# Moving a head's pair products from the start of the next step into the tail of its own step, in a kernel with a gated delta rule, a sparse graph mix and a mixture of experts

## The chip, the cores and the metric

The kernel runs on one core of a Trainium2 chip. The core has five engines that run their own instruction streams and meet only at semaphores: TensorE (PE: matmuls and transposes, PEld is its weight load), VectorE (DVE), ScalarE (ACT), GpSimd (POOL) and SyncE (SP), which here issues the DMAs. The metric is the time of one execution on the device in microseconds; the median of several runs counts.

## What is computed

x is (4, 256, 256). One decoder layer in three parts, each added to x after a layer norm:

```python
# 1: gated delta rule, 8 heads of 128, two Householder steps (j) per token
q, k, v = causal_conv_silu(x @ Wq), causal_conv_silu(x @ Wk), causal_conv_silu(x @ Wv)
q = l2norm(q) / sqrt(128); k = l2norm(k); beta = 2 * sigmoid(x @ Wb)
g = -exp(A_log) * softplus(x @ Wa + dt_bias)
for t in range(256):
    state = state * exp(g[t])
    for j in range(2):
        u = (v[t, j] - k[t, j] @ state) * beta[t, j]
        state = state + outer(k[t, j], u)
    o[t] = q[t] @ state
x = x + (rmsnorm(o) * norm_w * silu(x @ Wg)) @ Wo
# 2: top-k masked sigmoid of a similarity of ctx_512 (4, 256, 64), k = 76 of 256, symmetrised, mixed with norm(x)
# 3: feed forward: base expert plus the top 2 of 8 experts, hidden 704
```

## The kernel before, in words

The whole layer is float32 and runs in one program: `attention` (parts 1 and 2, about the first 630 us) and `feed_forward` (the rest). The diff touches `attention` alone.

**Chunks.** Time is cut into 4 chunks of 64 steps, that is 128 Householder rows; 4 sequences times 4 chunks make 16 tiles (BC) for each head. Inside a tile the recurrence is solved with the inverse of a 128x128 triangular matrix. Its strictly triangular part is `aT` (products of keys, times decays and beta, the array `dx`); its inverse is `TT`. The four 32x32 diagonal blocks of all 16 tiles are sent through device memory (`gather`: eight DMAs aT to a_blocks, then two a_blocks to `blk`), so that GpSimd can invert the 64 blocks side by side in 31 rounds of two instructions (`invert`, lines 1370 and 1373), and come back with `scatter` (inv to inverses, inverses to TT). TensorE then joins the blocks in five levels, each for two halves of the tiles (`p32`, `t32`, `x32`, `p64`, `t64`), and ScalarE copies each level out of PSUM.

**Steps.** The eight heads go through a software pipeline with four stages. In step s stage A works on head s (projections, convolution, norms, decays), B on head s-1 (inverse, transposes), C on head s-2 (the scan over four chunks) and E on head s-3 (output projection). There are 11 steps, 0 to 10. Each step has 12 slots and a place behind them, LAST; before the change it also had a place ahead of them, FIRST. A table, `FILL`, says which items of A, B and E stand in which place. The order in the code is the order on each engine; nothing reorders it.

**Items and banks.** An item is a group of matmuls into one of three PSUM banks (`bankB`) in rotation, so an item waits until the one three places before it in the table has been copied out (`bank_free`). `pair` n (8 of them for a head) makes the key and query products of two tiles; VectorE turns each into `aT` (line 1121) and `mq` (the masked query products, line 1126), 0.4 and 0.3 us. `dx`, `ex` are decays and `out` is the output projection, whose result VectorE adds to `acc` (line 1214) times `factor`, the inverse root mean square of the head's output. `factor` is made in three places: TensorE's `out_sums` (line 725) at the start of the step, VectorE's `out_rms` (lines 1204, 1206), GpSimd's `out_rms` (line 1300), and the first `out` item of the step waits for it.

**Slots.** Slot i has projection i (line 582, slots 0 to 9) on TensorE, convolution i-1 (line 1055, three instructions, slots 1 to 10) on VectorE, and one third of a scan chunk: products with the state S (line 683, slots 3, 6, 9), with TT (697, slots 1, 4, 7, 10), with the query and the state update (711 to 716, slots 2, 5, 8, 11). VectorE makes R (1154), U (1162, also printed R) and S (1169, 1171) between them. The selection of the top 76 of each row (`topk`, lines 1070 and 1072, 20 calls for a tile of rows) fills VectorE's holes in steps 2 to 8: calls 0 to 7 in slot 0, calls 8 to 19 in slot 11. `turn_blocks` (line 1144, X1 from TT) is in slot 9 and waits for the DMAs of `scatter`; `p32` in slot 10 needs X1. At the end of a step ScalarE squares the output (`out_square`, line 889) and VectorE gates it (`out_gate`, line 1197).

On GpSimd the step is: clear TT, reset `inv` (`unit`), copy the head's conv weights and make `gm` (`start`), `out_rms`, `invert`, and then, for the head in A, `dm`, beta into `dx`, `kn`, `sh` and `qE`.

Of the kernel before, what the change touches and what calls it, by code (L numbers as in the profile page):

```python
# [98 lines left out]
def four(kind):  # L99
# [62 lines left out]
def attention(nc, ctx, t, dram):  # L162
# [45 lines left out]
    mq = [sb(f"mq{i}", [P, BATCH, CH, STEPS]) for i in range(2)]  # L208
    gate = [sb(f"gate{i}", [P, T]) for i in range(2)]
# [46 lines left out]
    m8 = sb("m8", [P, 8])  # L256
    thr = t["thr"]
# [128 lines left out]
    def sync_program(sp):  # L386
# [34 lines left out]
        def tiles_out():  # L421
# [112 lines left out]
    def tensor_program(pe):  # L534
# [80 lines left out]
        def item(kind, n, X):  # L615
# [12 lines left out]
            if kind in ("pair", "vtok", "kend"):  # L628
# [1389 lines left out]
```

## Time and profile before

| | |
|---|---|
| time, median of 3 runs | 946.38 us (941.20, 946.38, 946.81) |
| the profiled execution, its time | 940.37 us |
| its span, first to last instruction | 938.3 us |
| PE busy | 835.7 us (89%) |
| DVE, ACT, POOL busy | 530.1, 390.9, 347.5 us |
| mean granted TensorE clock | 0.939 |
| share of PE in the chain that ended last | 72% |

The span is some 2 us shorter than the time of that execution. The granted clock of TensorE is a share of 2.4 GHz; 0.50 is the lower level, 1.2 GHz. Busy time of a group counts each instruction once; the idle time in brackets at a row is the time in which that engine had nothing running just before the row, with the work that ended it.

### The profile page before, as it was taken

What the parts mean: (1) busy time and instruction counts of PE and PEld (TensorE: products, weight loads), DVE (VectorE), ACT (ScalarE), POOL (GpSimd) and SP (SyncE); (2) the same over time, 40 slices, a digit from 0 to 9 for tenths busy, and PEclk for the clock granted to TensorE, in tenths of its full rate; (3) what the DMA queues carried; (4) which work ended last, traced back from release to release, by engine and by line L of the source; (5) the groups of instructions that cost most, each with busy time, mean ns of one, the idle gap of its engine ahead of it and who ended that gap; (6) DMA issues with size and microseconds to landing.
All of it is one profiled execution on the core that took longest, in us unless ns stands there. A gap on an engine that the chain in (4) does not pass through costs nothing.

```text
span 938.3 us, 16243 instructions
## 1 busy us (share of the span) xinstructions
PE 835.7 (89%) x5560; PEld 580.5 (62%) x5561; DVE 530.1 (56%) x1285; ACT 390.9 (42%) x839; POOL 347.5 (37%) x654
## 2 busy tenths in 40 slices
PE   3969999989999999899899876874999999999992
PEld 2343566756766756767667765663667667666761
DVE  4564757878878868878778755465511111111113
ACT  3536756545654554655555323202222222222220
POOL 0157368457456565563683580003330000000015
PEclk9788999999999999999999886897999999999997
DMA  7302230130031031021201301009563100110104
GB/s 204 78 12 56 69 85 1 24 80 12 13 80 23 7 74 22 14 68 24 51 1 24 83 9 29 1 1 384 215 228 129 34 28 28 34 34 22 34 25 127
DMA packets 102593, 57.88 MB, mean 62 GB/s; under 512 B 64192, under 2 KB 98048, under 8 KB 102528
## 3 DMA queue, kind: packets, MB, share of 16 engines
q1 hardware_dynamic: 99488, 51.62, 20.0%
q0 software_dynamic: 1536, 4.20, 1.4%
q10 hardware_dynamic: 1504, 1.20, 0.4%
q8 instruction: 39, 0.64, 0.3%
q14 instruction: 26, 0.21, 0.1%
HBM read 42.45 MB, written 14.55 MB: 61 GB/s over the span
## 4 chain that ended last, share of the span: by engine, by line
PE 72%; DVE 10%; ACT 5%; POOL 4%; issue 4%; DMA 3%; SPq 1%; ACTq 0%; POOLq 0%; DVEq 0%
PE bank L1599 16%; PE bank L582 11%; PE bank L1644 9%; PE bank L712 3%; PE bank L590 3%; PE bank L637 3%; DVE y L1055 3%; PE bank L746 2%; PE bank L716 2%; PE bank L711 2%; PE bank L697 2%; PE bank L1631 2%; PE bank L596 2%; PE bank L671 2%; PE bank L683 2%
## 5 line engine op out<-in xcount | busy, mean ns | idle before, releaser
L1055 DVE SCALAR_TENSOR_TENSOR y<-bank,cwh,y 128x510 f32<-128x510 f32 (+2 forms) x240 | 177.5, 743 | 82.5 <-ACT y L833 78.8
L582 PE MATMUL bank<-xnT,wbuf 128*128 128x512 f32 x320 | 164.8, 641 | 5.5 <-DVE y L1055 5.0
L1599 PE MATMUL bank<-f_wgu,f_xgT 128*128 x368 | 118.8, 466 | 0.0
L1858 DVE TENSOR_TENSOR f_act<-f_sg,bank 128x352 f32<-128x352 f32 x62 | 32.2, 521 | 139.8 <-PE bank L1599 135.1
L1370 POOL TENSOR_TENSOR term<-inv,blk 128x126 f32<-128x126 f32 (+22 forms) x248 | 87.4, 352 | 63.3 <-DMA blk<-a_blocks 44.5
L1933 POOL DMA_INDIRECT f_back<-slots_y,f_slot x16 | 15.4, 960 | 228.8 <-DMA slots_y<-f_yb 222.2
L582 PEld LDWEIGHTS bank<-xnT,wbuf 128*128 128x128 f32 x320 | 56.8, 197 | 67.4 <-issue 53.8
L1373 POOL TENSOR_TENSOR inv<-inv,term 128x126 f32<-128x126 f32 (+22 forms) x248 | 91.2, 368 | 19.4
L1706 ACT ACTIVATE f_sg<-bank 128x352 f32<-128x352 f32 x62 | 28.6, 463 | 158.7 <-PE bank L1599 158.7
L1644 PE MATMUL bank<-f_wdn,f_actT 128*128 (+1 forms) x372 | 91.5, 387 | 0.8 <-ACT f_actT L1719 0.8
L1599 PEld LDWEIGHTS bank<-f_wgu,f_xgT 128*128 128x128 f32 x368 | 66.2, 190 | 36.8 <-issue 7.6
L833 ACT ACTIVATE y<-bank,cwh 128x512 f32<-128x512 f32 x80 | 54.9, 686 | 75.1 <-PE bank L582 73.4
L1644 PEld LDWEIGHTS bank<-f_wdn,f_actT 128*128 128x128 f32 x372 | 67.9, 189 | 24.1 <-issue 11.3
L1315 POOL TENSOR_TENSOR dx<-dx,minus_beta 128x1024 f32<-128x1024 f32 x8 | 15.2, 1902 | 115.6 <-DVE beta_n L1105 115.6
L637 PE MATMUL bank<-kq 128*128 128x192 f32 x256 | 47.3, 342 | 8.5 <-DVE mq L1126 8.5
L712 PE MATMUL bank<-mq,R 128*128 128x64 f32 x256 | 48.2, 288 | 3.1 <-DVE R L1162 3.1
L637 PEld LDWEIGHTS bank<-kq 128*128 128x128 f32 x256 | 43.2, 197 | 11.1 <-DVE mq L1126 10.2
L932 ACT ACTIVATE vtok<-bank,kn 128x128 f32<-128x128 f32 x128 | 36.4, 369 | 32.3 <-PE bank L642 32.3
L1300 POOL TENSOR_TENSOR factor<-factor,masks 128x8 f32<-128x8 f32 x8 | 13.3, 1662 | 85.7 <-DVE factor L1206 85.7
L1599 PE MATMUL bank<-f_wgu,f_x2T 128*128 128x352 f32 x128 | 44.4, 494 | 0.4 <-DVE f_act L1858 0.4
L712 PEld LDWEIGHTS bank<-mq,R 128*128 128x128 f32 x256 | 40.1, 205 | 6.6 <-DVE R L1162 3.7
L596 PE MATMUL bank<-gm,masks 64*128 64x512 f32 x64 | 30.2, 747 | 12.7 <-ACT dx L872 7.2
(204 smaller groups left out, 1501.4 us busy)
## 6 DMA issues: line engine op xcount, KB each, us to landing
f_wgu<-in_exp_gu SPq DMA_DIRECT2D x8, 1408.0 KB, 8.7
f_wdn<-in_exp_dn SPq DMA_DIRECT2D x8, 640.0 KB, 9.3
blk<-a_blocks SPq DMA_DIRECT2D x16, 256.0 KB, 3.9
slots_x<-oT SPq DMA_DIRECT2D x24, 128.0 KB, 1.9
f_xg<-slots_x SPq DMA_DIRECT2D x24, 128.0 KB, 2.0
slots_y<-f_yb SPq DMA_DIRECT2D x23, 128.0 KB, 1.7
a_blocks<-aT SPq DMA_DIRECT2D x64, 32.0 KB, 1.6
inverses<-inv SPq DMA_DIRECT2D x16, 128.0 KB, 3.0
```

The lines of the kernel that those rows point to most:

```text
L582: last = mm(bankA[p % 2][:, :], wbuf[A.par][:, kt, wblk, :], xnT[:, kt, (p % 2) * 512:(p % 2 + 1) * 512], start=kt == 0, stop=kt == 1)
L596: return mm(bank[:, :], mask("rest" if kind == "dx" else "ones", i * STEPS, STEPS), gm[half_, :, :].rearrange("p n t -> p (n t)"), start=T ...
L637: last = mm(bank[:, c * (MU + STEPS):(c + 1) * (MU + STEPS)], kraw[:, 2 * n + c, :], kq[:, 2 * n + c, :], start=True, stop=True)
L712: last = mm(out, U[:, b, :], mq[par][:, b, c, :], start=c == 0, stop=True)
L833: a(y[p % 2][:, :, :].rearrange("p b t -> p (b t)"), bankA[p % 2][:, :], ACT.Copy, scale=cwh[A.par][:, cb, 3:4]).then_inc(evac_done, 1)
L932: last = a(vtok[B.par][:, b, c, :], bank[:, c * P:(c + 1) * P], ACT.Copy, scale=kn[:, b * CH + c:b * CH + c + 1])
L1055: v.scalar_tensor_tensor(out=y[p % 2][:, :, k:], in0=src[:, :, 0:SEQ - k], scalar=cwh[A.par][:, cb, 3 - k:4 - k], in1=y[p % 2][:, :, k:], ...
L1370: g.tensor_tensor(step_term, inv[:, 0:r, j:j + 1].to_broadcast([P, r, k]), blk[:, j:j + 1, j + 1:].to_broadcast([P, r, k]), ALU.mult).then ...
L1373: g.tensor_tensor(inv[:, 0:r, j + 1:], inv[:, 0:r, j + 1:], step_term, ALU.add).then_inc(inv_done if j == NB - 2 else inv_step, 1)
L1599: last = mm(gu[c][:, 0:FFH], xt[:, k, :], wgu[:, e, k, at:at + FFH], start=k == 0, stop=k == 1)
L1644: last = mm(dn[par][:, 0:HID], aT[0:rows, par, k, :], wdn[0:rows, e, k, :], start=k == 0, stop=k == FT - 1)
L1858: v.tensor_tensor(av[:, par, half * FFH:(half + 1) * FFH], sg[:, half, :], gu[2 * half + 1][:, 0:FFH], ALU.mult).then_inc(f_act, 1)
```

## The change

The pair products of a head no longer open the next step. They stand in the head's own step: pairs 0 and 1 in slot 10, 2 and 3 in slot 11, and 4 to 7 in LAST, between the level products of the head ahead. `aT` has two buffers, since the level products of one head and the pair products of the next are now interleaved. The masked decays, which had the array `dm`, are written straight into one of three rotating `mq` buffers and multiplied in place. `gather` stands at the end of a head's own step. The decays' second half `ex` moves to slot 1; the squares and norms move earlier, and VectorE's norm sum and beta from slot 10 to slot 8. `turn_blocks` moves from slot 9 to slot 7, the levels up to `x32` 0 one place ahead. The selection makes 14 calls in slot 0 and the last 6 after LAST. On GpSimd `start`, `unit` and `clear` of the next inverse stand in the step before, and `out_rms` stands inside `invert`, ahead of round 12 (`RMS_AT`). Step 0 and step 8 have entries of their own.

```diff
-FIRST, LAST = "first", "last"
-FILL = {FIRST: {"B": [("pair", n) for n in range(BC // 2)]},
-        0: {"A": [("dx", 0), ("dx", 1), ("ex", 0), ("ex", 1)]},
-        1: {"E": [("out", 0)], "B": [("vtok", 0)]},
+LAST = "last"
+FILL = {0: {"A": [("dx", 0), ("dx", 1)]},
+        1: {"A": [("ex", 0), ("ex", 1)], "E": [("out", 0)], "B": [("vtok", 0)]},
...
-        8: {"B": [("kend", 1)]},
-        9: {"B": [("gate", 0)]},
-        10: {"B": [("p32", 0), ("p32", 1)], "E": [("out", 3)]},
-        11: {"B": [("t32", 0), ("t32", 1), ("kend", 2)]},
-        LAST: {"B": [("x32", 0), ("x32", 1), ("gate", 1), ("p64", 0), ("p64", 1), ("t64", 0), ("t64", 1)]}}
+        8: {"B": [("kend", 1), ("gate", 0)]},
+        9: {"B": [("p32", 0), ("p32", 1), ("kend", 2)]},
+        10: {"B": [("t32", 0), ("t32", 1)], "A": [("pair", 0), ("pair", 1)]},
+        11: {"B": [("x32", 0)], "A": [("pair", 2), ("pair", 3)], "E": [("out", 3)]},
+        LAST: [("B", [("x32", 1)]), ("A", [("pair", 4), ("pair", 5)]), ("B", [("p64", 0), ("p64", 1), ("gate", 1)]),
+               ("A", [("pair", 6), ("pair", 7)]), ("B", [("t64", 0), ("t64", 1)])]}
+
+STEP_0 = {0: {}, 1: {}, 3: {"A": [("dx", 0), ("dx", 1), ("ex", 0), ("ex", 1)]}}
...
+RMS_AT = 12
+TOP_FIRST = 14
...
         def step(A, B, C, E):
-            if B:
-                gather(B)
...
+            if A:
+                gather(A)
...
-                if A and 6 <= slot < 10:
-                    norm(A, slot - 6)
+                if A and slot in (5, 7):
+                    norm(A, slot - 5)
+                    norm(A, slot - 4)
...
-                if A and 5 <= slot <= 10:
-                    square(A, slot - 5)
+                if A and slot in (4, 6, 8):
+                    square(A, slot - 4)
+                    square(A, slot - 3)
...
-                    topk(tiles[0], 0, 8)
+                    topk(tiles[0], 0, TOP_FIRST)
...
-                if B and slot == 9:
+                if B and slot == (7 if A else 10):
                     turn_blocks(B)
-                if A and slot == 10:
+                if A and slot == 8:
                     norm_sum(A, 0)
                     fold_beta(A)
...
             fill(LAST)
+            if A and tiles:
+                topk(tiles[0], TOP_FIRST, 2 * ROUNDS)
...
             for j in range(NB - 1):
+                if j == RMS_AT and E:
+                    out_rms(E)
...
             if B:
-                clear(B)
-                unit(B)
-            if A:
-                start(A)
-            if E:
+                invert(B, E)
+            elif E:
                 out_rms(E)
-            if B:
-                invert(B)
             if A:
...
                 decays(A)
+                if A.h + 1 < HEADS:
+                    start(Head(A.h + 1, (A.h + 1) % 2, (A.h + 1) // 2))
+                if A.h:
+                    unit(A)
                 fold_beta(A)
                 norm(A)
                 scalars(A)
                 q_decay(A)
+                clear(A)
```

TensorE at the boundary of two steps, before. L669 is `x32`, L590 the gate, L671 `p64`, L673 `t64`, L637 the pairs, L725 `out_sums`, L596 the decays, L582 projection 0:

```order
L669 MATMUL bank<-masks,TT 64x64 x16
L590 MATMUL bank<-xnT,wg 128x512 x2
L671 MATMUL bank<-XP,aT 64x64 x16
L673 MATMUL bank<-TT,XP 64x64 x16
L637 MATMUL bank<-kq 128x192 x16
L725 MATMUL bank<-osq,masks 32x256 x4
L596 MATMUL bank<-gm,masks 128x512 x4
L582 MATMUL bank<-xnT,wbuf 128x512 x2
```

The same place after. L693 is `x32`, L652 the pairs, L770 `out`, L626 the norms, L695 `p64`, L605 the gate, L697 `t64`, L749 `out_sums`, L611 the decays:

```order
L693 MATMUL bank<-masks,TT 64x64 x8
L652 MATMUL bank<-kq 128x192 x4
L770 MATMUL bank<-wo,og 128x256 x2
L626 MATMUL bank<-osq,masks 32x128 x8
L693 MATMUL bank<-masks,TT 64x64 x8
L652 MATMUL bank<-kq 128x192 x4
L695 MATMUL bank<-XP,aT 64x64 x16
L605 MATMUL bank<-xnT,wg 128x512 x2
L652 MATMUL bank<-kq 128x192 x4
L697 MATMUL bank<-TT,XP 64x64 x16
L749 MATMUL bank<-osq,masks 32x256 x4
L611 MATMUL bank<-gm,masks 128x512 x2
```

The 16 pair matmuls that stood between `t64` and `out_sums` are in groups of four ahead of `t64`, so `out_sums` now follows `t64` directly.

GpSimd at the start of a step with all four stages, before. L1300 is `out_rms`, L1370 and L1373 are the rounds of `invert`:

```order
L1347 MEMSET TT 128x16x32
L1354 MEMSET inv 128x512
L1358 AFFINE_SELECT inv<-inv 64x512 x2
L1281 COPY cwh<-cw 128x20
L1287 TENSOR_TENSOR gm<-g_sb,masks 128x512
L1300 TENSOR_TENSOR factor<-factor,masks 128x8
L1370 TENSOR_TENSOR term<-inv,blk 128x31
L1373 TENSOR_TENSOR inv<-inv,term 128x31
```

After. L1322 is `out_rms`, L1395 and L1398 the rounds:

```order
L1398 TENSOR_TENSOR inv<-inv,term 128x6x21
L1395 TENSOR_TENSOR term<-inv,blk 128x120
L1398 TENSOR_TENSOR inv<-inv,term 128x6x20
L1322 TENSOR_TENSOR factor<-factor,masks 128x8
L1395 TENSOR_TENSOR term<-inv,blk 128x133
L1398 TENSOR_TENSOR inv<-inv,term 128x7x19
```

`out_rms` has moved behind twelve of the 31 rounds, so it also stands behind their wait for `blk`.

VectorE between slots 7 and 9, before. L1144 is `turn_blocks`, L1171 makes S, L1154 R, L1055 are convolutions, L1214 the addition of `out`:

```order
L1171 SCALAR_TENSOR_TENSOR S<-S,sh,bank 128x128 x4
L1055 SCALAR_TENSOR_TENSOR y<-bank,cwh,y 128x2x254
L1055 SCALAR_TENSOR_TENSOR y<-bank,cwh,y 128x2x253
L1132 TENSOR_TENSOR kend<-bank,sh 128x4x128
L1055 SCALAR_TENSOR_TENSOR y<-bank,cwh,y 128x2x255
L1154 SCALAR_TENSOR_TENSOR R<-bank,sh,vtok 128x128 x4
L1055 SCALAR_TENSOR_TENSOR y<-bank,cwh,y 128x2x254
L1055 SCALAR_TENSOR_TENSOR y<-bank,cwh,y 128x2x253
L1144 STREAM_TRANSPOSE X<-TT 32x512 x2
```

After. L1167 is `turn_blocks`, L1194 makes S, L1079 are convolutions, L1237 the addition of `out`, L1107 opens the norm sum:

```order
L1237 SCALAR_TENSOR_TENSOR acc<-bank,factor,acc 128x256 x2
L1167 STREAM_TRANSPOSE X<-TT 32x512 x2
L1079 SCALAR_TENSOR_TENSOR y<-bank,cwh,y 128x2x255
L1194 SCALAR_TENSOR_TENSOR S<-S,sh,bank 128x128 x4
L1079 SCALAR_TENSOR_TENSOR y<-bank,cwh,y 128x2x254
L1079 SCALAR_TENSOR_TENSOR y<-bank,cwh,y 128x2x253
L1155 TENSOR_TENSOR kend<-bank,sh 128x4x128
L1107 STREAM_TRANSPOSE turned<-bank 128x512
```

`turn_blocks` now stands ahead of convolution 7 and of the third update of S.

## Rows read from the trace of the kernel before

**Rows 1.** The page: its first line, its part 1 and the clock of its part 2.

```profile
span 938.3 us, 16243 instructions
...
PE 835.7 (89%) x5560; PEld 580.5 (62%) x5561; DVE 530.1 (56%) x1285; ACT 390.9 (42%) x839; POOL 347.5 (37%) x654
...
PEclk9788999999999999999999886897999999999997
```

**Rows 2.** Windows (length, busy us of PE, PEld, DVE, ACT, POOL, clock, DMA): steps 4, 5, 8.

```profile
258.20:323.90 65.70, 62.78 (x533) 44.42 (x533) 54.58 (x127) 37.50 (x74) 38.42 (x77) 1.00 0.18 37
323.90:391.20 67.30, 64.41 (x533) 44.91 (x533) 54.50 (x127) 37.42 (x74) 38.43 (x76) 0.97 0.17 37
524.40:598.00 73.60, 54.16 (x436) 45.35 (x437) 38.98 (x118) 21.44 (x43) 23.95 (x64) 0.74 0.16 38
```

**Rows 3.** Timeline of PE, step 5 (start, length, what).

```profile
320.31 2.22 PE L637 MATMUL bank<-kq 128*128 128x192 f32 x12
323.86 3.52 PE L637 MATMUL bank<-kq 128*128 128x192 f32 x20 [1.33 <-DVE mq L1126]
...
330.97 1.12 PE L596 MATMUL bank<-gm,masks 64*128 64x512 f32 x2 [1.11 <-ACT dx L872]
...
343.39 1.05 PE L683 MATMUL bank<-S,kT 128*128 128x128 f32 x8
...
368.75 1.05 PE L683 MATMUL bank<-S,kT 128*128 128x128 f32 x8
...
385.67 2.04 PE L673 MATMUL bank<-TT,XP 64*64 64x64 f32 x32
```

**Rows 4.** Timeline of DVE, step 5.

```profile
327.41 0.42 DVE L1121 TENSOR_TENSOR aT<-bank,dx 128x256 f32<-128x256 f32 x1
...
328.58 0.42 DVE L1070 MAX8 m<-simw 128x8 f32<-128x256 f32 x1
...
336.37 0.75 DVE L1055 SCALAR_TENSOR_TENSOR y<-bank,cwh,y 128x510 f32<-128x510 f32 x1 [3.89 <-ACT y L833]
...
339.06 0.87 DVE L1214 SCALAR_TENSOR_TENSOR acc<-bank,factor,acc 128x256 f32<-128x256 f32 x2
...
341.43 0.88 DVE L1169 COPY S<-bank 128x128 f32<-128x128 f32 x4 [0.32 <-PE bank L716]
...
372.80 1.43 DVE L1144 STREAM_TRANSPOSE X<-TT 32x512 f32<-32x512 f32 x2
...
389.32 1.28 DVE L1197 SCALAR_TENSOR_TENSOR og<-oT,normw,gate 128x1024 f32<-128x1024 f32 x1 [0.82 <-ACT osq L889]
```

**Rows 5.** Timeline of POOL, step 5.

```profile
328.74 1.64 POOL L1300 TENSOR_TENSOR factor<-factor,masks 128x8 f32<-128x8 f32 x1 [3.63 <-DVE factor L1206]
336.64 0.24 POOL L1370 TENSOR_TENSOR term<-inv,blk 128x31 f32<-128x31 f32 x1 [6.26 <-DMA blk<-a_blocks]
...
346.67 0.42 POOL L1370 TENSOR_TENSOR term<-inv,blk 128x133 f32<-128x133 f32 x1
...
363.52 0.23 POOL L1373 TENSOR_TENSOR inv<-inv,term 128x16 f32<-128x16 f32 x1
```

**Rows 6.** The chain that ended last, step 2 (start, length, what).

```profile
164.88 4.28 DMA inverses<-inv
...
172.96 0.70 DVE X L1144
```

**Rows 7.** Timeline of PE, steps 8 and 9.

```profile
533.71 1.97 PE L712 MATMUL bank<-mq,R 128*128 128x64 f32 x8 [2.79 <-DVE R L1162]
...
575.43 1.92 PE L663 MATMUL bank<-X,aT 32*32 32x32 f32 x64 [7.20 <-DVE X L1144]
...
596.90 0.64 PE L725 MATMUL bank<-osq,masks 128*32 128x256 f32 x8 [1.63 <-ACT osq L889]
```

**Rows 8.** Window of step 8, columns as in rows 2.

```profile
538.00:540.00 2.00, 1.88 (x9) 1.54 (x8) 0.41 (x3) 1.14 (x4) 1.61 (x6) 0.50 0.93 314
```

**Rows 9.** Timeline of PE, step 1.

```profile
71.08 3.75 PE L596 MATMUL bank<-gm,masks 64*128 64x512 f32 x6 [5.10 <-POOL gm L1287]
```

More of the change, by code:

```diff
@@ L130, in items_at @@
     if step == 0:
-        table = FILL[0] if place == FIRST_DECAYS else {} if place == 0 else table
-    return table.items()
+        table = STEP_0.get(place, table)
+    if step == HEADS:
+        table = STEP_8.get(place, table)
+    return table.items() if isinstance(table, dict) else table
 def tiles_of(step):
@@ L256, in attention @@
     m8 = sb("m8", [P, 8])
+    aT1 = sb("aT1", [P, BATCH, CH, MU])
+    aT = [aT0, aT1]
     thr = t["thr"]
@@ L644, in item, with level_ready @@
                 return
+            level_ready(kind, n, h)
+            for k in range(BC // 2):
+                last = level(kind, n, X, k, bank)
+            last.then_inc(b_mm, 1)
+        def level_ready(kind, n, h):
             if kind == "p32":
@@ L674, in item, with level @@
-            last.then_inc(b_mm, 1)
+        def level(kind, n, X, k, bank):
+            par, m = X.par, n * (BC // 2) + k
+            a_m, t_m = aT[par][:, m // CH, m % CH, :], TT[par][:, m // CH, m % CH, :]
+            cols = slice(k * STEPS, (k + 1) * STEPS)
+            if kind == "p32":
+                for g in range(2):
+                    src, out = slice(2 * g * NB, (2 * g + 1) * NB), slice((2 * g + 1) * NB, (2 * g + 2) * NB)
+                    last = mm(bank[out, k * NB:(k + 1) * NB], a_m[src, out], X1[src, m, :], start=True, stop=True)
+            elif kind == "t32":
+                for g in range(2):
+                    src, out = slice((2 * g + 1) * NB, (2 * g + 2) * NB), slice(2 * g * NB, (2 * g + 1) * NB)
+                    last = mm(bank[out, k * NB:(k + 1) * NB], P32[src, m, :], t_m[src, src], start=True, stop=True)
+            elif kind == "x32":
+                last = nc.tensor.transpose(bank[0:64, cols], t_m[0:64, 0:64], ident[0:64, 0:64])
+            elif kind == "p64":
+                last = mm(bank[64:128, cols], a_m[0:64, 64:128], XP[0:64, m, :], start=True, stop=True)
+            else:
+                last = mm(bank[0:64, cols], XP[64:128, m, :], t_m[64:128, 64:128], start=True, stop=True)
+            return last
@@ L711, in scan @@
                         mm(out, S[:, b, :], qE[par][:, b, c, :], start=True, stop=False)
-                    last = mm(out, U[:, b, :], mq[par][:, b, c, :], start=c == 0, stop=True)
+                    last = mm(out, U[:, b, :], mq[h % 3][:, b, c, :], start=c == 0, stop=True)
                 last.then_inc(o_mm, 1)
@@ L756, in fill @@
                             item(kind, n, stages[stage])
-            fill(FIRST)
             if E:
@@ L1282, in start @@
                           cw[:, :, :, :].rearrange("p h a k -> p h (a k)")[:, h, :]).then_inc(cwh_done, 1)
-            if some(4 * h):
+            if h:
                 item_done(pool, "ex", h - 1, 1)
```

66 lines of the change are left out of this document (26 added, 40 removed).

## The prediction

> **What bounds the kernel now.** I read the page first, for which engine is near its limit [rows 1]: PE is busy 89% of the span and DVE only 56%. Then the windows by step, for where PE is not busy [rows 2]: the steps with all stages last 65.7 and 67.3 us in turn, mean 66.5, with PE busy for 62.8 and 64.4, so there are some 2.9 us to be had in each of them. Step 8, which has no projections, is another matter: 73.6 us, of which PE is busy 54 at a mean clock of 0.74. Last the timelines, to see who waits at the boundary of two steps. The gaps of PE there are 1.33 us, where a pair product waits for its bank, and 1.11 us, where a decay does [rows 3]. So the middle of the kernel is bound by TensorE with 96% filled, and a reordering can gain little there and lose much. The feed forward part is not touched.
>
> Below, S is the moment at which PE ends the last `t64` of a step: 387.71 (385.67 + 2.04), and 320.3 one step earlier, where the pairs begin [rows 3].
>
> **The pairs move ahead of S: nothing at first.** Their work is the same, 2.22 + 3.52 = 5.7 us [rows 3], and the two steps' starts shift by it. Between level products their banks have time to be read, so the wait of 1.33 us should go. What is late next is `out_sums`: it follows `t64` directly now, and needs ScalarE's square of the output, which ScalarE does only after the copy of the last `t64`. In step 9, the one step of before with no pairs in front, PE waited 1.63 us for just that [rows 7]. DVE's gate waits for the same square, and starts at 389.32, that is S + 1.6 [rows 4]. So 1.6 us comes for 1.33 us that goes. The 1.11 us of the decays should go too, because a projection now stands between `dx` and `ex`.
>
> **The inverse starts too late for its new place.** The inverse's round trip begins with the last `aT`. In step 5 that ends at 327.83 (327.41 + 0.42) [rows 4], and the first round starts at 336.64 [rows 5]: 8.8 us for `gather` and `blk`. The last pairs stand just ahead of `t64` (2.0 us) in the new order and their copy takes 0.4, so the last `aT` ends at about S - 1.6, and the first round starts at S + 7.2. Round 12 (133 wide) is 346.67 - 336.64 = 10.0 us further on [rows 5]. There GpSimd now makes `factor`, 1.64 us [rows 5]: it is ready at S + 18.9. Before, it was made ahead of the inverse, in time that GpSimd spent waiting for `blk` anyway (idle 6.26 us before the first round [rows 5]), at 330.4.
>
> When does VectorE want it? Gate from S + 1.6 to S + 2.8 (the 1.28 us row), 0.6 us for `out_rms`, then 14 calls of the selection in place of 8. Eight calls ran from 328.58 to 332.48 (336.37 less the idle time of 3.89) [rows 4], 0.49 us each, so 14 take 6.9 us and end at S + 10.3. One convolution, U and two convolutions lie between that and the addition of `out` 0: 339.06 - 336.37 = 2.7 us [rows 4], S + 13.0. Two costs follow. U comes to PE at S + 11.7; with two projections and the items of slot 1 done PE is there some 2 us earlier (estimate), a wait that the next one swallows. And DVE stops dead at the addition from S + 13.0 to S + 18.9, with convolution 1 and S queued behind it. Addition 0.8, convolution 0.7, S 0.9: S is ready at S + 21.3, and the third slot's product (line 683) can start. All of the earlier work of PE is long done by then.
>
> From that product to the end of `t64` PE ran without holes in step 5: 387.71 - 343.39 = 44.3 us, and the 5.7 us of pairs are added to it: the next S is 21.3 + 44.3 + 5.7 = 71.3 us after this one, against 66.5: **+4.8 us a step** if the clock stays up.
>
> **The clock.** After a wait of 2.79 us in step 8 PE ran at 0.50 of its clock [rows 7, 8]: eight product rows took 1.97 us, and the lower level, 1.2 GHz, was still on at 540. That is 6.3 us at half rate with 3.1 us lost; with what lies behind 540 I take 3.4. In the steps of now, the two small gaps cost 1.7 us every second step (clock 0.97 against 1.00 [rows 2]). The new waits, 1.6, 2 and up to 5 us, come within 21 us in each step. Some of the slow stretch falls into time in which PE waits anyway, so I take half of 3.4: 73.0 us a step, **+6.5**. The Trainium skill, page "TensorE: Matmul & The Clock Gate", section "What's actually happening", says that the throttled state is the default and that only activity releases it. By that rule PE would come out of every one of these waits at the low level, and the whole 3.4 us would be lost in each step: 74.7. No run of before shows such a wait inside a full step.
>
> Steps 3 to 7 have both a head in A and one in E: 5 x 6.5 = **+32**.
>
> **The way back.** From the last `aT` to X1 before: 8.8, then the rounds until 363.75, 27.1 us, then the DMAs, 172.96 - 164.88 = 8.1 and an issue of 0.6 [rows 5, 6]: 44 to 45 us. Slot 9 was reached at 372.80, 45.0 after 327.83 [rows 4], so this was just hidden. Now `turn_blocks` stands two slots earlier; VectorE reaches it about S + 42 in a held step and TT lands at S + 43.5 to 45 with the 1.6 us of `factor` added. That wait is small and mostly covered, because X1 is not used before slot 9, which PE reaches at 21.3 + (368.75 - 343.39) + 1.9 for the gate moved ahead of it = S + 48.6 [rows 3].
>
> **Step 2** has no head in E and so no hold, and there the round trip itself sets the length: X1 comes at 44 after the last `aT`, S 3.1 us later, then 387.71 - 368.75 = 19.0 from slot 9's product, less 1.9 for the gate, plus 5.7 for pairs, less 1.5 from S back to the last `aT`: 44 + 24.4 = 68.5, against the mean of 66.5, and 1.7 for low clock after the wait at `turn_blocks`: **+4**.
>
> **Steps 0 and 1.** `gm` is ready a step ahead: the wait of 5.10 us for it [rows 9] goes, and head 0's pairs can be done some 2 us sooner. But step 1 is bound by the round trip of head 0, and X1 in slot 7 holds convolutions 7 to 9 and the pairs behind it, where before only one convolution came after it: **+1**, bounds -5 and +3.
>
> **Step 8.** `factor` holds S in the same way. Before, S was made from about 537.5 (533.71 + 1.97, and as much again for the state update), 9.6 after the end of the pairs at 527.9 (524.4 + 3.5) [rows 2, 3, 7]; now from S + 19.7, +10. Only 6 instead of 12 calls of the selection stand on the way to slot 9, -2.9, and `turn_blocks` has U ahead of it, +0.7: **+8**, bounds +2 (no hold) and +10. The 7.20 us wait for X1 [rows 7] stays, since the selection and not the inverse ends last before it.
>
> Selection calls after LAST (2.9 us) fit between the last pair and the gate's wait. The array `mq` in three buffers, `aT` in two and the earlier squares and norms cost nothing: the same instructions, ahead of a user that comes later.
>
> **Sum**: 1 + 4 + 32 + 8 = +45 us on the profiled execution's 940.4: 985. The median of the three runs is 946.4, 6 above it, so I add 1: **986 us**. A change within 1% could not be told from none here.
>
> **Rivals.**
> 1. The hold is as forecast and each wait costs the full slow stretch (the skill's rule, as a mechanism of this kernel: PE resumes at 0.50 as in rows 8): 5 x 8.2 + 1 + 5 + 10 = +57, 997. For it: both long waits of step 8 went that way. Against: part of it falls into waits.
> 2. `factor` does not hold (if `blk` lands early, or the addition comes late). Then the round trip with `turn_blocks` in slot 7 sets the step: 44 + 1.7 + 24.4 = 70.1, 5 x 3.6 = 18, plus 5 and 3: 967.
> 3. Faster. The two gaps of PE go, its clock stays at 1.00, step 1 loses its 5.10 us, and step 8 has its inverse early: 7 x 1.3 + 6 x 0.85 + 6 + 8 = -28, 912. It decides at one point: `blk` has to be there by S - 1 and not S + 7.2, so that `factor` is ready when VectorE comes to it. For it: DVE and POOL have 40% and more to spare on average. Against: the last pairs are issued 2 us before S, and 8.8 us of DMA follow in every step of before.
> 4. Gains of steps 0, 1 and 8 and smaller holds cancel: within 1%.
>
> **How the numbers follow.** Forecast 0.45 (975 to 996), rival 1 0.20 (to 1003), rival 2 0.15 (958 to 974), rival 4 0.07, rival 3 0.10, worse than 1003 0.03. The range 958 to 1003 leaves out 0.20. Faster 0.10, same 0.07, slower 0.83.
>
> **What would show it.** Right: DVE's longest waits in steps 3 to 7 are at the addition of `out` 0 (line 1237) for GpSimd's `factor`, some 5 to 6 us each; PE waits 4 to 5 us at line 707 in slot 3 for S, and 1.6 us at line 749 for ScalarE; step length 71 to 75 us; low clock after slot 3. Wrong: `factor` ready before S + 13, a step below 67 us, or a first round earlier than 8 us after the last `aT`. The forecast fails most easily if VectorE's 14 calls or PE's path are already later than the hold, which would make the hold free.

## The result, and the profile after

The changed kernel takes 977.59 us (median of 4 runs, 973.46 to 981.35), the kernel before 945.95 in the same comparison. The ratio is 1.034, 95% interval 1.029 to 1.039: slower, by 31.6 us. The forecast was 986 with 958 to 1003.

The page of after, its first line, part 1 and clock, against [rows 1]:

```profile
span 976.3 us, 16235 instructions
...
PE 838.5 (86%) x5560; PEld 587.1 (60%) x5561; DVE 521.5 (53%) x1285; ACT 389.3 (40%) x839; POOL 341.6 (35%) x654
...
PEclk9999598998998998989989969797899999999997
```

The span is 38.0 us longer and PE is busy for only 2.8 us more, so the loss is in the main waiting. (The profiled execution of before was one of its faster ones, 940.4 us against a median of 946, which is why 38.0 is more than the 31.6 of the medians.) `t64` now ends a step, so S itself is the border. Windows of after, steps 3, 5 and 8 and two short stretches of step 5, columns as in [rows 2]:

```profile
203.28:274.52 71.24, 65.39 (x532) 46.42 (x532) 53.31 (x126) 37.30 (x73) 37.38 (x76) 0.93 0.17 34
346.05:418.35 72.30, 65.02 (x532) 46.40 (x532) 53.41 (x126) 37.43 (x73) 37.41 (x76) 0.93 0.17 34
561.33:631.30 69.97, 46.95 (x404) 39.78 (x404) 35.93 (x108) 23.28 (x46) 23.86 (x63) 0.76 0.16 38
367.64:370.64 3.00, 3.00 (x13) 3.00 (x14) 2.88 (x7) 0.03 (x1) 2.60 (x6) 0.50 0.00 0
370.64:373.64 3.00, 3.00 (x11) 1.51 (x11) 1.64 (x3) 2.21 (x6) 2.53 (x7) 0.77 0.00 0
```

The mean of steps 3 to 7 is (561.33 - 203.28) / 5 = 71.6 us. Before, from one end of `t64` to the next, it was 66.8. Three timelines of step 5 of after, with S = 346.05, answer to [rows 3, 4, 5]. PE:

```profile
343.97 2.08 PE L697 MATMUL bank<-TT,XP 64*64 64x64 f32 x32
347.67 0.71 PE L749 MATMUL bank<-osq,masks 128*32 128x256 f32 x8 [1.63 <-ACT osq L913]
...
357.89 1.00 PE L736 MATMUL bank<-mq,R 128*128 128x64 f32 x8
...
367.64 2.08 PE L707 MATMUL bank<-S,kT 128*128 128x128 f32 x8 [5.65 <-DVE S L1192]
```

DVE:

```profile
344.08 0.42 DVE L1145 TENSOR_TENSOR aT<-bank,dx 128x256 f32<-128x256 f32 x1
...
357.43 1.52 DVE L1079 SCALAR_TENSOR_TENSOR y<-bank,cwh,y 128x508 f32<-128x508 f32 x2
365.27 0.88 DVE L1237 SCALAR_TENSOR_TENSOR acc<-bank,factor,acc 128x256 f32<-128x256 f32 x2 [6.31 <-POOL factor L1322]
366.06 0.74 DVE L1079 SCALAR_TENSOR_TENSOR y<-bank,cwh,y 128x510 f32<-128x510 f32 x1
366.72 0.87 DVE L1192 COPY S<-bank 128x128 f32<-128x128 f32 x4
```

POOL:

```profile
353.61 0.24 POOL L1395 TENSOR_TENSOR term<-inv,blk 128x31 f32<-128x31 f32 x1 [17.21 <-DMA blk<-a_blocks]
...
363.12 0.44 POOL L1398 TENSOR_TENSOR inv<-inv,term 128x120 f32<-128x120 f32 x1
363.52 1.65 POOL L1322 TENSOR_TENSOR factor<-factor,masks 128x8 f32<-128x8 f32 x1
```

Read backwards, the three are one chain. PE stands for 5.65 us at the product of slot 3 until VectorE has made S. VectorE has stood for 6.31 at the addition of `out` 0, two instructions ahead of S, until GpSimd has `factor`. GpSimd made `factor` directly behind round 11 (no idle time in front of it), and its first round had waited for `blk`, whose data left with the last `aT` at 344.50. When PE resumes, eight products take 2.08 us at clock 0.50, where they took 1.05 in [rows 3]. The list of waits of after (total us, times, longest) says how often; the 6.6 us at line 736 are in step 2:

```profile
POOL term L1395 <- DMA blk<-a_blocks: 119.2, 8, 17.2
DVE acc L1237 <- POOL factor L1322: 36.2, 8, 7.1
PE bank L707 <- DVE S L1192: 27.7, 7, 5.7
PE bank L736 <- DVE R L1185: 11.5, 3, 6.6
```

**Where the 38.0 us lie.** Before, a step's own work began when the pairs were done. These two rows of PE before, and 527.96 for step 8 (524.44 + 3.52), give the starts; 595.28 ends step 8:

```profile
123.40 5.47 PE L637 MATMUL bank<-kq 128*128 128x192 f32 x32
...
190.87 3.52 PE L637 MATMUL bank<-kq 128*128 128x192 f32 x20 [1.79 <-DVE mq L1126]
...
593.23 2.05 PE L673 MATMUL bank<-TT,XP 64*64 64x64 f32 x32
```

| stretch | before | after | more | forecast |
|---|---|---|---|---|
| up to the end of step 1 | 128.87 | 134.85 | +6.0 | +1 |
| step 2 | 65.5 | 68.4 | +2.9 | +4 |
| steps 3 to 7 | 333.6 | 358.05 | +24.5 | +32 |
| step 8 | 67.3 | 70.0 | +2.7 | +8 |
| steps 9, 10 and feed forward | 343.0 | 345.0 | +2.0 | 0 |

Each column is one execution, and two rows of it scatter from one execution to the next. The last row, from the last `t64` to the end, is 343.0 to 343.2 in e1, e2, e3 and e9 and 347.8 and 348.7 in e8 and e12 (the runs below), all of which have the same instructions there as after; so its +2.0 need not be the change's. The first row has up to 3.5 us of such scatter (see steps 0 and 1 below).

### The profile page after: what moved, and what is told of

It reads as the page before. It is cut to its first block, busy times and chain, and to the rows that moved or that the text cites. A ratio compares the mean times of both kernels' runs of the same rounds, so it can differ in the third digit from the quotient of the medians.

```text
span 976.3 us, 16235 instructions
## 1 busy us (share of the span) xinstructions
PE 838.5 (86%) x5560; PEld 587.1 (60%) x5561; DVE 521.5 (53%) x1285; ACT 389.3 (40%) x839; POOL 341.6 (35%) x654
## 3 DMA queue, kind: packets, MB, share of 16 engines
q1 hardware_dynamic: 99488, 51.62, 19.4%
## 4 chain that ended last, share of the span: by engine, by line
PE 64%; DVE 8%; POOL 7%; DMA 5%; issue 3%; SPq 1%; ACT 1%; DVEq 0%; ACTq 0%
PE bank L1626 15%; PE bank L1671 8%; PE bank L597 8%; PE bank L652 4%; PE bank L707 3%; POOL inv L1398 3%; PE bank L605 3%; DMA blk<-a_blocks 3%; POOL term L1395 3%; PE bank L736 2%; PE bank L735 2%; PE bank L721 2%; PE bank L770 2%; PE bank L1658 2%; PE bank L740 2%
## 5 line engine op out<-in xcount | busy, mean ns | idle before, releaser
L1079 DVE SCALAR_TENSOR_TENSOR y<-bank,cwh,y 128x510 f32<-128x510 f32 (+2 forms) x240 | 177.6, 743 | 41.4 <-ACT y L857 37.4
L1395 POOL TENSOR_TENSOR term<-inv,blk 128x126 f32<-128x126 f32 (+22 forms) x248 | 87.4, 352 | 137.5 <-DMA blk<-a_blocks 119.2
L597 PEld LDWEIGHTS bank<-xnT,wbuf 128*128 128x128 f32 x320 | 61.2, 208 | 71.5 <-issue 58.1
L1398 POOL TENSOR_TENSOR inv<-inv,term 128x126 f32<-128x126 f32 (+22 forms) x248 | 91.1, 367 | 19.4
L1733 ACT ACTIVATE f_sg<-bank 128x352 f32<-128x352 f32 x62 | 28.6, 463 | 161.1 <-PE bank L1626 161.1
L707 PE MATMUL bank<-S,kT 128*128 128x128 f32 x192 | 32.6, 322 | 31.2 <-DVE S L1192 27.7
L707 PEld LDWEIGHTS bank<-S,kT 128*128 128x128 f32 x192 | 28.7, 225 | 41.5 <-DVE S L1192 32.4
L652 PE MATMUL bank<-kq 128*128 128x192 f32 x256 | 50.2, 341 | 3.0 <-DVE mq L1149 3.0
L1145 DVE TENSOR_TENSOR aT<-bank,dx 128x256 f32<-128x256 f32 x64 | 27.3, 428 | 45.2 <-PE bank L652 44.6
L1237 DVE SCALAR_TENSOR_TENSOR acc<-bank,factor,acc 128x256 f32<-128x256 f32 x64 | 27.6, 477 | 42.5 <-POOL factor L1322 36.2
L652 PEld LDWEIGHTS bank<-kq 128*128 128x128 f32 x256 | 42.3, 193 | 9.0 <-issue 3.8
```

The lines of the kernel that those rows point to most:

```text
L597: last = mm(bankA[p % 2][:, :], wbuf[A.par][:, kt, wblk, :], xnT[:, kt, (p % 2) * 512:(p % 2 + 1) * 512], start=kt == 0, stop=kt == 1)
L652: last = mm(bank[:, c * (MU + STEPS):(c + 1) * (MU + STEPS)], kraw[:, 2 * n + c, :], kq[:, 2 * n + c, :], start=True, stop=True)
L707: last = mm(bankC[0][:, b * P:(b + 1) * P], kT[par][:, b, c, :], S[:, b, :], start=True, stop=True)
L1079: v.scalar_tensor_tensor(out=y[p % 2][:, :, k:], in0=src[:, :, 0:SEQ - k], scalar=cwh[A.par][:, cb, 3 - k:4 - k], in1=y[p % 2][:, :, k:], ...
L1395: g.tensor_tensor(step_term, inv[:, 0:r, j:j + 1].to_broadcast([P, r, k]), blk[:, j:j + 1, j + 1:].to_broadcast([P, r, k]), ALU.mult).then ...
L1398: g.tensor_tensor(inv[:, 0:r, j + 1:], inv[:, 0:r, j + 1:], step_term, ALU.add).then_inc(inv_done if j == NB - 2 else inv_step, 1)
```

## The experiments

Each table of steps below is read as above, from the ends of `t64`: the length is the mean of steps 3 to 7. Ratios are to the kernel before on the same chip.

### One and two at a time: factor and turn_blocks

`e1_rms_first` puts `factor` ahead of the inverse again, `e2_turn_slot8` puts `turn_blocks` behind convolution 7, `e3_rms_first_turn_slot8` does both. The last two lines of the diff are e2's, the others e1's.

```diff
             for j in range(NB - 1):
-                if j == RMS_AT and E:
-                    out_rms(E)
...
         def step(A, B, C, E):
+            if E:
+                out_rms(E)
             if B:
                 invert(B, E)
-            elif E:
-                out_rms(E)
...
-                if B and slot == (7 if A else 10):
+                if B and slot == (8 if A else 10):
```

> The changed kernel with GpSimd's out_rms ahead of the inverse, as before the change; all else as changed. Theory H (the place of out_rms holds VectorE at the addition of out 0): the 6 us wait at line 1237 goes, S is ready about S + 15.4 in place of S + 21.3, and steps 3 to 7 fall from 71.6 us until the next limit. Theory R says what that limit is: the round trip of the inverse with turn_blocks in slot 7, 8.8 + 27.1 + 8.7 + 24.4 = 69 us, so only 2.6 us a step come back, and VectorE waits at turn_blocks for the DMA in every step; with step 8's 6 us the time is some 958 us. Rival P (the pair products among the level products cost TensorE by themselves, the hold is free): within 1% of 977.

> The changed kernel with turn_blocks in slot 8 in place of 7 (behind convolution 7 and S); out_rms stays at round 12. H: steps 3 to 7 stay at 71 to 72 us, since VectorE is held earlier in the step and X1 is not the last thing that TensorE waits for. R: steps 1 and 2, where there is no hold, get 2 to 4 us shorter each. Together 970 to 975 us. If R alone made the steps long, every step would fall by 2 us: about 963.

> Both edits: out_rms ahead of the inverse, turn_blocks in slot 8. With H and R both true they add more than singly: steps 3 to 7 at 66 to 68 us, steps 1 and 2 shorter by 2 to 4 us, step 8 by 6: about 945 us, level with the kernel before the change. If the round trip does not bind, the same as e1.

| | time | ratio | a step | what VectorE waits for in a step |
|---|---|---|---|---|
| after | 977.6 | 1.034 (1.029 to 1.039) | 71.6 | `factor`, 5 to 6 us |
| e1 | 954.6 | 1.012 (1.006 to 1.018) | 68.8 | X1, 3.8 to 5.3 us |
| e2 | 974.8 | 1.033 (1.027 to 1.038) | 71.4 | `factor`, 5 to 6 us |
| e3 | 939.7 | 0.997 (0.993 to 1.001) | 65.2 | neither |

After was compared on another occasion, so for it the ratios count more. The hold by `factor` is worth 2.2% (20 us by the ratios) with `turn_blocks` in slot 7, and 974.8 - 939.7 = 35 us with it in slot 8. The place of `turn_blocks` is worth at most 3 us with the hold and 15 without it. The parts do not add up, because the hold hides the wait for X1: VectorE loses its 5 us at `factor` and finds X1 there when it reaches slot 7. VectorE of e1 in step 4 (its S is 272.10) and of e3 (265.98), no idle time at the addition, and the wait at X1 in e1 alone:

```profile
284.92 0.87 DVE L1237 SCALAR_TENSOR_TENSOR acc<-bank,factor,acc 128x256 f32<-128x256 f32 x2
...
312.89 1.43 DVE L1167 STREAM_TRANSPOSE X<-TT 32x512 f32<-32x512 f32 x2 [4.12 <-DMA TT<-inverses]
```

```profile
278.80 0.87 DVE L1237 SCALAR_TENSOR_TENSOR acc<-bank,factor,acc 128x256 f32<-128x256 f32 x2
...
307.91 1.42 DVE L1167 STREAM_TRANSPOSE X<-TT 32x512 f32<-32x512 f32 x2
```

The third update of S stands behind X1 in e1, and PE waits 0.8 to 2.3 us for it. The window of e3, step 4, is the kernel without either:

```profile
265.98:331.09 65.11, 61.91 (x532) 44.19 (x532) 52.95 (x126) 37.37 (x73) 37.48 (x76) 1.00 0.18 38
```

65.1 us at full clock is 1.7 less than the mean before, and 0.6 less than a step of before at full clock (65.7, [rows 2]). That is what the rest of the change is worth here, the moved pairs together with the earlier squares, norms and decays, which were not taken apart. Steps 1 and 2 of e3 give 6.5 us back (step 1 ends at 132.14, step 2 takes 68.7 us). In step 2 I had expected 2 to 4 us from `turn_blocks` in slot 8; e2 and e3 took 69.0 and 68.7 there, after 68.4. X1 was not what ended last in that step (see step 2 below).

### The hold alone, in the kernel before

`e4_before_rms_at_12` changes only the place of `factor` in the kernel before.

```diff
         def invert(B, E):
             for j in range(NB - 1):
+                if j == 12 and E:
+                    out_rms(E)
...
         def step(A, B, C, E):
...
-            if E:
-                out_rms(E)
             if B:
-                invert(B)
+                invert(B, E)
+            elif E:
+                out_rms(E)
```

> The kernel before the change with one edit: out_rms inside invert, ahead of round 12. H by itself: factor is ready at 336.6 + 10.0 + 1.6 = 348.3 on step 5's times and the addition stood at 339.1, so VectorE is held 9 us; S comes at 350.7 where TensorE wanted it at 343.4, +7 us in steps 3 to 7, and some 10 us in step 8: 946 + 45 = 990 us, up to 1005 if TensorE's clock falls after each wait. Rival (VectorE's hole of 3.9 us and later holes take it in): under 960.

1000.3 us, ratio 1.064 (1.056 to 1.072), 74.9 us a step, of the size expected. Here the inverse begins later against the start of the step, so VectorE waits longer. First VectorE, then PE, step 4:

```profile
289.37 0.88 DVE L1214 SCALAR_TENSOR_TENSOR acc<-bank,factor,acc 128x256 f32<-128x256 f32 x2 [9.82 <-POOL factor L1300]
```

```profile
291.74 2.08 PE L683 MATMUL bank<-S,kT 128*128 128x128 f32 x8 [7.89 <-DVE S L1169]
```

### How much earlier is enough: round 6, with turn_blocks in slot 7 and 8

`e9_rms_at_6` and `e12_rms_at_6_turn_slot8` leave `factor` inside the inverse, six rounds sooner; the last two lines are e12's alone:

```diff
-RMS_AT = 12
+RMS_AT = 6
...
-                if B and slot == (7 if A else 10):
+                if B and slot == (8 if A else 10):
```

> The kernel after with factor's last step ahead of round 6 of the inverse and not ahead of round 12, which is 5.5 us sooner by the trace of after (357.99 against 363.52). Theory of the hold: the wait at the addition falls from 6.3 to about 1 us, S comes 5 us sooner, and the time is near that with the step ahead of the inverse (954.6), plus 5 x 0.5: 955 to 960. Rival (standing inside the inverse costs as such, 1.65 us in the round trip and a wait between VectorE and GpSimd): it keeps more than half of the 23 us, 966 or more.

e9 took 971.8 us, ratio 1.032 (1.026 to 1.038): my theory missed by 12 us and the rival's number was right. Its mechanism was not settled by that. VectorE of e9 in step 4 (S = 274.40), PE where VectorE's wait reaches it, and the window:

```profile
287.23 0.87 DVE L1237 SCALAR_TENSOR_TENSOR acc<-bank,factor,acc 128x256 f32<-128x256 f32 x2
...
316.79 1.43 DVE L1167 STREAM_TRANSPOSE X<-TT 32x512 f32<-32x512 f32 x2 [5.76 <-DMA TT<-inverses]
```

```profile
320.09 1.53 PE L707 MATMUL bank<-S,kT 128*128 128x128 f32 x8 [2.78 <-DVE S L1194]
```

```profile
274.40:345.84 71.44, 66.58 (x532) 46.57 (x532) 53.05 (x126) 37.46 (x73) 37.38 (x76) 0.93 0.16 34
319.40:325.40 6.00, 5.31 (x78) 4.50 (x79) 5.60 (x16) 2.18 (x5) 1.39 (x1) 0.61 0.01 3
```

The hold is gone and the step is as long as with it. The same 5 us are now lost at X1, in slot 7, and behind PE's wait there its clock is 0.61 in the mean. The rounds take 28.6 us and not the 27.1 of e1, because `factor` is still among them. So the question was whether the second limit alone explains e9, and e12 takes it away:

> The kernel after with factor's last step ahead of round 6 and turn_blocks in slot 8. The first move alone gave 971.8 us, the second alone 974.8. Theory (two limits of the same length, 71.5 us a step, each of which hides the other): with both off the step falls to TensorE's own 65.1 us, as with factor ahead of the inverse (939.7); the inverse is 1.65 us longer here, and X1 comes at S + 42.3 where VectorE wants it at S + 41.9, so at most 0.4 us a step more: 939 to 943. Rival (standing inside the inverse costs as such): the step stays near 71 us, 965 or more.

946.8 us, ratio 1.000 (0.997 to 1.003), 67.0 us a step. The rival (standing inside the inverse costs as such, 965 or more) falls: 25 us went with a move on VectorE alone (30 by the ratios). What standing inside costs is at most the distance to e3, 7 us, or 3 by the ratios. The theory is 4 us short of the time; the kernel before was itself 3 us slower on this chip (947.3 against 944.1 for e3). What it lacks is in the steps: I had allowed 0.4 us each, and in two of them X1 still came 1.3 and 1.7 us too late for slot 8. Those took 68.4 and 68.8 us, where the shortest is 65.6.

### An earlier start of the inverse

`e8_pairs_early` moves pairs 6 and 7 only:

```diff
-        LAST: [("B", [("x32", 1)]), ("A", [("pair", 4), ("pair", 5)]), ("B", [("p64", 0), ("p64", 1), ("gate", 1)]),
-               ("A", [("pair", 6), ("pair", 7)]), ("B", [("t64", 0), ("t64", 1)])]}
+        LAST: [("B", [("x32", 1)]), ("A", [("pair", 4), ("pair", 5), ("pair", 6), ("pair", 7)]),
+               ("B", [("p64", 0), ("p64", 1), ("gate", 1), ("t64", 0), ("t64", 1)])]}
```

> The kernel after with one move: pairs 6 and 7 ahead of p64 and t64. factor stays inside the inverse. Theory of the hold (the start of the inverse decides when factor is ready): the last aT comes 5 us sooner, first round and factor too, so the wait of 6.3 us at the addition shrinks to 1 or 2: 4 us by 6 steps less, 953 to 958. Rival (the time goes to turn_blocks in slot 7 or to the low clock, not to the hold): the start of the inverse moves but the steps keep their 71.6 us, 972 to 978.

949.0 us, ratio 1.006 (1.002 to 1.009), better than expected: 66.3 us a step. The last `aT` ends at S - 5.5 in place of S - 1.6, and both limits move at once. Step 4 of e8, VectorE (S = 266.30):

```profile
280.70 0.88 DVE L1237 SCALAR_TENSOR_TENSOR acc<-bank,factor,acc 128x256 f32<-128x256 f32 x2 [1.50 <-POOL factor L1322]
...
305.42 0.70 DVE L1167 STREAM_TRANSPOSE X<-TT 32x512 f32<-32x512 f32 x1 [2.28 <-DMA TT<-inverses]
```

1.50 and 2.28 us are left of 6.3 and 5.8. This one shift of 3.9 us gave back 2.8% (27 us by the ratios), more than `factor` alone.

`e5_rms_turn_pairs_early` joins it to e3's two moves.

> The kernel after with three moves: factor's last step ahead of the inverse on GpSimd, turn_blocks in slot 8, and pairs 6 and 7 ahead of the joining levels p64 and t64 instead of between them. The first two alone gave 939.7 us. Theory (the round trip of the inverse has slack once the hold is gone, apart from steps 1 and 2 where X1 ends last): the last aT comes 5 us sooner, which can only be worth something in step 1 and 2, 3 us each at most: 934 to 937. Rival (the round trip still sets every full step): 5 us by 6 steps less, about 915 to 925. Second rival: with nothing between p64 and t64 but the gate, t64 waits for ScalarE's copy, 1 us a step: 945 to 948.

934.8 us, ratio 0.991 (0.988 to 0.994), 65.3 us a step, as e3. The round trip has slack there, as expected, and the gain is in step 2: 66.1 us against 68.7. Step 1 gave nothing, though it ends at 129.85 against 132.14: the last `aT` of head 0 had been 2.9 us sooner in this execution (61.28 against 64.16), with the same work in front of it, and from there to the end of step 1 it is 68.6 against 68.0.

### The selection and out_sums

`e6_top8_rms_inside` is after, and `e7_rms_first_top8` is e1, each with

```diff
-TOP_FIRST = 14
+TOP_FIRST = 8
```

> The kernel after with 8 calls of the selection in slot 0 and 12 after LAST; factor stays inside the inverse, turn_blocks in slot 7. Theory: the hold at the addition swallows whatever slot 0 gains, and the inverse isn't behind the gate here, so nothing changes: 974 to 980. Rival (six calls cost PE 2 us a step at U whatever comes later): 965 to 969. Second rival (more calls after LAST delay factor's first part on VectorE, as in the kernel with factor ahead of the inverse, where eight calls cost 20 us): 985 or more.

> The kernel after with factor's last step ahead of the inverse and with 8 calls of the selection in slot 0 and 12 after LAST, in place of 14 and 6. With the first move alone it was 954.6 us. Theory: the six calls stood ahead of U and held PE some 1.5 to 2 us a step, a wait that shows now that the hold does not swallow it: 5 x 2 less in steps 3 to 7, 943 to 948. Rival: the twelve calls after LAST (5.9 us) delay VectorE's gate and R of the next step by as much as slot 0 gains: 954 to 958.

e6: 981.9 us, ratio 1.040 (1.034 to 1.046), 2 us above the range I gave, with the same 71.6 us a step as after. The hold does swallow what slot 0 gains. Step 8 is 3.7 us longer (73.7 us), which I had not expected. e7: 975.3 us, ratio 1.036 (1.031 to 1.042), 20.7 us worse than e1, which neither theory had. GpSimd of e7 in step 4 (S = 272.15):

```profile
278.07 1.64 POOL L1322 TENSOR_TENSOR factor<-factor,masks 128x8 f32<-128x8 f32 x1 [15.58 <-DVE factor L1229]
279.67 0.24 POOL L1393 TENSOR_TENSOR term<-inv,blk 128x31 f32<-128x31 f32 x1
```

Six more calls after LAST delay VectorE's gate and its part of `factor` by 2.4 us, and with `factor` ahead of the inverse the first round no longer waits for `blk` but for `factor`: S + 7.5 in place of 6.2. X1 is late in e1 already, so the 1.3 us goes straight into the step; the mean step is 2.8 us longer (71.6), and in step 4 PE's clock fell to 0.50 behind the wait. This is the price of the old place of `factor`, and the reason why it can look right to move it inside.

`e10_sums_behind_decays` and `e11_sums_behind_decays_top8` build on e5; the last two lines are e11's alone:

```diff
-            if E:
-                out_sums(E)
...
                 fill(slot)
+                if E and slot == 0:
+                    out_sums(E)
...
-TOP_FIRST = 14
+TOP_FIRST = 8
```

> The best kernel so far (934.8 us: factor ahead of the inverse, turn_blocks in slot 8, pairs 6 and 7 early) with TensorE's out_sums behind the dx decays of slot 0 and not ahead of them. Theory: the wait of 1.63 us for ScalarE's square shrinks to 0.5, in the seven steps that have both: 1.1 us each, 5 x 1.1 = 5.5 less, 927 to 931. Rival: factor comes 0.6 us later and the inverse, U and the rest with it, so that PE waits as much later on: 933 to 937.

> The kernel of the run before with 8 calls of the selection in slot 0 and 12 after LAST. VectorE sat idle 4.4 us ahead of the gate there, room for nine calls of 0.49 us, so six more fit. Theory: the gate is not delayed and U comes 2.9 us sooner, which takes PE's wait of 1.13 us for it: 5 x 1.1 less than the run before, 922 to 926. Rival (the gate is delayed as with late pairs, the inverse starts behind it): 930 or more.

e10: 937.5 us, ratio 0.991 (0.988 to 0.995), nothing gained. PE in step 4 shows its rival right in part: the wait for the square falls by 1.06 to 0.57, and the one for U, 1.13 in e5, is 1.58. Steps 5 and 6 take 65.1 us, no less than steps 3 to 5 of e5; where the other 0.6 us go was not traced.

```profile
264.00 0.64 PE L749 MATMUL bank<-osq,masks 128*32 128x256 f32 x8 [0.57 <-ACT osq L913]
...
273.90 1.35 PE L736 MATMUL bank<-mq,R 128*128 128x64 f32 x8 [1.58 <-DVE R L1185]
```

e11: 925.4 us, ratio 0.979 (0.974 to 0.984), the fastest kernel of the study. The mechanism is the one expected: the gate on VectorE of e11 still waits for the square, so the six calls cost nothing, PE's wait for U is gone, and PE is busy for 62.3 of 63.3 us. That the number was met is luck in part. I had counted from a run before of 927 to 931, and it took 937.5; the gain over it is 12 us and not 5.5: 1.8 us a step in the mean of steps 3 to 7, and 5.1 in step 2 (61.2 against 66.3), which the theory did not have. VectorE, then the window of that step:

```profile
255.98 1.28 DVE L1220 SCALAR_TENSOR_TENSOR og<-oT,normw,gate 128x1024 f32<-128x1024 f32 x1 [1.43 <-ACT osq L913]
```

```profile
254.37:317.65 63.28, 62.26 (x534) 44.50 (x534) 53.12 (x126) 37.26 (x73) 37.44 (x76) 1.00 0.19 39
```

Whether e11 needs the move of `out_sums` at all was not tried.

## Why the prediction was right, and where it was not

**The hold.** Right in place and size. Predicted for a full step: last `aT` S - 1.6 (measured -1.55), VectorE at the addition at S + 13.0 (358.95, S + 12.9), `factor` at S + 18.9 (S + 19.1 in step 5, 18.05 in the mean of five), the product of slot 3 at S + 21.3 (21.6, mean 20.5), PE's wait at line 749 of 1.6 us (1.63 in each of steps 3 to 9). The mean comes sooner because `blk` took 7.6 to 8.1 us from the last `aT` in four of the five steps (9.1 in step 5), and not the 8.8 read from one step in [rows 4, 5].

**The clock.** The term is mis-sized. I took 1.7 us a step on top of 71.3. From the product of slot 3 to the next S after took 71.6 - 20.5 = 51.1, against 50.0 at full clock: 1.1. Together with the 0.8 above, that is 73.0 down to 71.6; with 66.7 before, where I took 66.5, five steps cost 24.5 in place of 32. The low clock behind PE's first wait costs nothing, since PE only arrives later at the hold. Rival 1 (every wait costs its whole slow stretch) is ruled out for that reason.

**The wait for U.** Wrong in steps 3 to 7. I had PE wait some 2 us for it; in step 5 line 736 runs at 357.89 with no idle time. PE was itself late: from S + 3 to S + 6, behind `out_sums`, it ran at 0.59 of its clock. The step said that the hold would swallow this wait, so no number hung on it. In e3, at full clock, it is there, with 1.12 us. In step 2 it is PE's longest wait (below).

**The way back.** The prediction called the wait at X1 small and covered, and put a step without the hold at 70.1 us (rival 2). e9 is that kernel: 71.4 us in step 4, and 72.2 in the mean of five. The forecast worked because both limits are nearly equal; it did not say that each hides the other, which is why my expectation of e9 failed.

**Step 2.** Forecast 68.5 and 1.7 for the clock, measured 68.4: near in size, and by luck, for the wait named is not the one that was there. X1 came 0.19 us late. PE's longest wait in the whole step was for U, 6.64 us, and behind it PE ran with less than 1.5 us of holes to the end. VectorE, PE and two DMA issues of after, then one of before (SPq is the queue in which SyncE issues DMAs):

```profile
141.42 0.43 DVE L1094 MAX8 m<-simw 128x8 f32<-128x256 f32 x1 [7.93 <-DMA simw<-similarities]
```

```profile
149.58 1.97 PE L736 MATMUL bank<-mq,R 128*128 128x64 f32 x8 [6.64 <-DVE R L1185]
```

```profile
136.31 1.13 SPq L461 DMA_DIRECT2D blk<-a_blocks  x2
137.49 0.58 SPq L433 DMA_DIRECT2D simw<-similarities  x1
```

```profile
117.43 0.34 SPq L419 DMA_DIRECT2D simw<-similarities  x1
```

The selection's first input is loaded by SyncE, and in the new order that load is issued behind `gather`, 2.6 us after the border of the step; before, it was issued 11.4 us ahead of the border (128.87), and VectorE never waited for it. So the 14 calls began at S + 6.6, and U was made behind them. The round trip is the second limit of the step, of the same length: in e6 and e7, with 8 calls, PE's wait for U is 3.7 and 3.5 us, X1 is 4.0 and 4.2 us late, and the step takes 68.1 both times. No run moves the load alone; in e11 (8 calls, pairs early, slot 8) the step takes 61.2.

**Steps 0 and 1.** The sign of the balance was wrong: +6.0, outside my bounds of -5 and +3. I let the early pairs pay for `turn_blocks` in slot 7. They do come sooner, as forecast: the last `aT` of head 0 ends at 64.06 and not 66.43. But from there to the end of step 1 it is 70.8 us in place of 62.4. In step 1 `turn_blocks` blocks VectorE for 16.5 us, with convolutions 7 to 9 behind it. VectorE of after, and PE, waiting for the same X1:

```profile
107.03 1.43 DVE L1167 STREAM_TRANSPOSE X<-TT 32x512 f32<-32x512 f32 x2 [16.52 <-DMA TT<-inverses]
```

```profile
108.61 1.06 PE L687 MATMUL bank<-X,aT 32*32 32x32 f32 x32 [12.46 <-DVE X L1167]
```

The end of step 1 by itself misleads, since the same work in front of it scatters: the last `aT` of head 0 came between 60.70 (e12) and 64.21 (e9), and the 64 short products of step 0 (line 567) took 3.62 us in after and 2.05 in e1 and in before. Counted from that `aT`, step 1 ends after 69.9 to 70.8 us in the six runs with `turn_blocks` in slot 7 (after, e1, e6 to e9) and after 68.0 to 69.0 in the six with it in slot 8 (e2, e3, e5, e10 to e12). So its place costs some 2 us of the 8.4. Pairs 6 and 7 ahead of `p64` give nothing here (e8 70.8, e5 68.6). The other 6 us were not traced; what is known is that they lie behind X1 (from there to the end of the step 25.5 us in e2 against 19.4 before).

**Step 8.** +2.7 in place of +8. The hold is there as predicted (7.09 us, the product of slot 3 at S + 19.6), but X1's product comes only 5.2 us later against the start of the step than before (613.99 - 561.33 = 52.7 against 575.43 - 527.96 = 47.5), and from there to the end it is 17.3 in place of 19.9. The error is in charging the hold in full. e1, which is after without the hold, takes 63.7 us for step 8, so the hold costs 6.3 there and not 10, and all the rest of the change gives 3.6 us back where I took 2.2. What shortens the last stretch was not tested.

Against a forecast of +45 on the profiled execution it is +38: 5.0 too little at the start, 1.1, 7.5 and 5.3 too much in steps 2, 3 to 7 and 8, and 2.0 in the rest, which is within the scatter shown above.

## What to carry to other kernels

Before an instruction goes into an iterated loop on another engine, ask what that loop waits for at its start. Its new time is that wait plus the rounds, and whoever adds it up must name what is queued behind its reader. Where two chains of nearly the same length close a loop, undoing either alone shows less than it is worth (by the ratios 1 us for e2, 2 for e9 and 20 for e1, but 32 and 35 for both, in e12 and e3); test them singly and together, and look for the shift that shortens both (here the last input of the round trip, 3.9 us sooner for 27 us). An instruction moved in a queue also moves what stands behind it there: behind `gather` the selection's load is issued 14 us later against its step, and step 2 waited for it. A reordered step should be judged when its waits are gone: the same idea is 3.4% slower in one order and 2.1% faster in another.

## What the runs showed of the hardware

The wait of 1.63 us at `out_sums` is the same in after and in e3, and PE's work around it too. In after the granted clock of the 3 us behind it (S + 3 to S + 6) was 0.69, 0.61, 0.59, 0.69, 0.63 in steps 3 to 7; in e3 it was 1.00 in all of them, and 0.50 only in step 8. Windows of e3, that stretch in step 4 and in step 8:

```profile
268.98:271.98 3.00, 3.00 (x14) 1.73 (x12) 2.79 (x11) 2.97 (x6) 1.63 (x1) 1.00 0.98 226
529.72:532.72 3.00, 3.00 (x12) 2.53 (x11) 2.79 (x11) 0.65 (x2) 1.63 (x1) 0.50 0.97 238
```

So the length of a wait does not settle by itself whether PE comes out of it at 1.2 GHz. The Trainium skill, page "TensorE: Matmul & The Clock Gate", section "What's actually happening", says that the throttled state is the default and activity releases it; the long waits here agree (0.50 behind 5.65 us). The prediction took from it that PE comes out of every wait at the low level, which is more than it says, and the 1.63 us did so in after and not in steps 3 to 7 of e3. What differs between the two kernels ahead of the wait was not isolated.

The clock also makes equal steps unequal. Windows of e1, steps 3 and 4, the same instructions:

```profile
201.52:272.10 70.58, 66.71 (x532) 46.62 (x532) 53.04 (x126) 37.34 (x73) 37.46 (x76) 0.93 0.17 35
272.10:339.81 67.71, 63.83 (x532) 44.72 (x532) 52.98 (x126) 37.45 (x73) 37.50 (x76) 0.97 0.17 36
```

2.87 us apart, with 2.88 us of difference in PE's busy time: a wait of 1.68 us behind X1 in the first was followed by the lower level, one of 1.14 in the second was not.
